# A state-space layer beside a mixture of experts: expert pairs move into scan group 0, slot scatters go by column, and POOL makes seven of the products dt*u*B

## What is computed

```
# ssm: 512 channels, 16 states each
xz = xn @ in_proj.T;  x, z = split(xz)            # no gate function on z
x  = silu(causal_conv4(x) + conv_b)
dt, Bm, Cm = split(x @ x_proj.T, [128, 16, 16])
dt = softplus(dt @ dt_proj.T + 2 * dt_proj_b)
state[l] = exp(dt * A) * state[l-1] + dt * Bm * x # per channel and state
y  = sum_n(state * Cm) + x * D;  out = (y * z) @ out_proj.T
# moe: 64 experts, top 8 of softmax(xn @ gate.T), weights not renormalised
h = silu(xn @ w1[e].T) * (xn @ w3[e].T);  out += c[e] * (h @ w2[e].T)
```

## Time and profile before

| | us |
|---|---|
| median of 3 runs (508.74 to 509.46) | 508.83 |
| profiled execution | 509.57 |
| its span, first to last instruction | 507.4 |
| PE busy | 430.4 |
| DVE busy | 430.5 |
| ACT busy | 246.7 |
| POOL busy | 293.8 |
| mean granted PE clock, share of full | 0.915 |

### The profile page before, as it was taken

One profiled execution on the slowest core, in us unless ns is written; L12 is line 12 of the kernel. 1 busy time (PEld: TensorE's weight loads), 2 busy tenths in 40 slices (PEclk: granted clock), 3 DMA queues, 4 the chain that ended last, 5 costly groups with the idle time before them and its releaser, 6 DMA issues.

```text
span 507.4 us, 9083 instructions
## 1 busy us (share of the span) xinstructions
PE 430.4 (85%) x2136; PEld 304.8 (60%) x2136; DVE 430.5 (85%) x646; ACT 246.7 (49%) x469; POOL 293.8 (58%) x260
## 2 busy tenths in 40 slices
PE   1986969038889999999999997999999949887996
PEld 1732424011157888788787885788878835454754
DVE  5288999989989888898789795888888889999994
ACT  1245367032435655555455665565555632454560
POOL 2000678777756766666545434566766537777772
PEclk9989979655569999999999997999999989997999
DMA  8999399722249999999999997899999944333432
GB/s 278 428 427 424 126 381 398 268 94 103 103 135 310 314 330 348 333 316 314 317 324 312 324 322 268 257 319 326 327 329 331 327 152 122 103 115 106 124 105 88
DMA packets 55417, 132.29 MB, mean 261 GB/s; under 512 B 7616, under 2 KB 11712, under 8 KB 53344
## 3 DMA queue, kind: packets, MB, share of 16 engines
q1 hardware_dynamic: 49248, 115.21, 65.6%
q0 software_dynamic: 6144, 16.79, 10.3%
HBM read 88.39 MB, written 43.58 MB: 260 GB/s over the span
## 4 chain that ended last, share of the span: by engine, by line
SPq 26%; POOL 18%; PE 15%; issue 15%; DVE 12%; DMA 12%; ACT 1%; POOLq 1%; DVEq 0%; ACTq 0%
POOL slot_x L329 13%; SPq L260 10%; SPq L261 6%; DMA slot_x<-bc 5%; DVE bank L572 5%; DMA slot_y<-x_sb 5%; PE bank L1004 4%; SPq L236 4%; SPq L264 3%; SPq L267 3%; PE bank L1015 2%; PE bank L1031 2%; DVE dbu L565 2%; PE bank L974 2%; DVE hc L578 2%
## 5 line engine op out<-in xcount | busy, mean ns | idle before, releaser
L337 POOL TENSOR_TENSOR dbu<-dtu,bc 128x512 f32 x80 | 101.9, 1274 | 99.5 <-DVE bank L572 86.8
L329 POOL DMA_INDIRECT slot_x<-x_sb,slot x64 | 68.8, 1075 | 68.2 <-DMA slot_x<-bc 49.0
L572 DVE TENSOR_TENSOR_SCAN bank<-dA,dbu 128x512 f32<-128x512 f32 x68 | 90.1, 1325 | 10.4 <-POOL dbu L337 1.7
L756 ACT ACTIVATE dA<-dt_sb,a_neg 128x512 f32<-128x512 f32 (+1 forms) x68 | 49.4, 727 | 66.3 <-DVE bank L572 66.1
L572 DVE TENSOR_TENSOR_SCAN bank<-bank,dbu 128x512 f32<-128x512 f32 x60 | 73.8, 1230 | 5.8
L782 ACT COPY x_sb<-bank 128x512 f32<-128x512 f32 x66 | 38.6, 585 | 75.0 <-DMA slot_y<-x_sb 72.7
L1004 PE MATMUL bank<-x_sb,wring 128*128 128x128 f32 x528 | 67.9, 283 | 0.1
L1004 PEld LDWEIGHTS bank<-x_sb,wring 128*128 128x128 f32 x528 | 64.8, 199 | 1.1 <-issue 0.5
L578 DVE TENSOR_TENSOR hc<-bank,bc 128x512 f32<-128x512 f32 x90 | 61.8, 686 | 1.4 <-POOL hp L344 0.3
L756 ACT ACTIVATE bank<-dt_sb,a_neg 128x512 f32 x60 | 41.7, 695 | 9.6 <-DVE bank L572 9.6
L592 DVE SCALAR_TENSOR_TENSOR gt<-th,bank 128x256 f32<-128x256 f32 x65 | 27.0, 416 | 22.5 <-ACT th L776 22.1
(11 more groups left out here) (180 smaller groups left out, 796.5 us busy)
## 6 DMA issues: line engine op xcount, KB each, us to landing
wring<-w_moe SPq DMA_DIRECT2D x64, 384.0 KB, 4.5
slot_y<-x_sb SPq DMA_DIRECT2D x66, 256.0 KB, 4.8
slot_x<-bc SPq DMA_DIRECT2D x16, 1024.0 KB, 22.1
xT<-w_moe SPq DMA_DIRECT2D x32, 384.0 KB, 4.5
win<-w_moe SPq DMA_DIRECT2D x32, 384.0 KB, 4.7
bc<-bc_dram SPq DMA_DIRECT2D x8, 1024.0 KB, 15.9
xg<-slot_x SPq DMA_DIRECT2D x32, 256.0 KB, 4.6
xT<-slot_x SPq DMA_DIRECT2D x16, 256.0 KB, 4.9
```

Of the source, the lines that this page charges most:

```text
L329: pool.indirect_dma_start(slot_x, bass.IndirectOffsetOnAxis(ap=slot[:, t * K + k:t * K + k + 1], axis=0), x_sb[:, t, :], None).then_inc(sc ...
L337: nc.gpsimd.tensor_tensor(dbu[:, j], at(dtu, g), bc[:, bass.ds(n, 1), 0].rearrange("p a l -> p (a l)"), ALU.mult).then_inc(dbu_ok, 1)
L572: nc.vector.tensor_tensor_scan(H[:], dA[:, j] if fall is None else fall, dbu[:, j], 0.0, ALU.mult, ALU.add).then_inc(scan_ok, 1)
L756: nc.scalar.activation(dA[:, j] if fall is None else fall, at(dt_sb, g), ACT.Exp, scale=a_neg[:, bass.ds(g, 1), bass.ds(n, 1)].rearrange(" ...
```

## The change

`EARLY` is 16, `GT` is G - 3 = 5. What it does, stage by stage:

- **Scatters** go by slot column: k = 7 for all 8 tiles first (the lowest slots), then k = 6, and so on. Each column has a semaphore; when it has landed, POOL raises `cols_ok`.
- **Early pairs.** DVE and PE work out for the first 16 pairs how many columns each needs (`low`, `lowest`, `reach`, `need`: four small operations on DVE, two on PE). `load_early` on SP reads that number into a register and waits for that many columns, then loads the rows. Worked out from the reference's inputs, pairs 0 to 15 need 1, 2, 3, 4, 4, 4, 4, 5, 5, 6, 6, 6, 6, 6, 7 and 7 columns.
- **Group 0** gets 12 pairs: from state 4 on, one `hidden` per scan step (`AHEAD0` = 4). It has one `sum_states` product on PE per scan step, three in pair step 0 and one in each later one. After scatter 36, and after every fourth from there, POOL makes the product dt*u*B for an odd state (`spread_odd`, states 1 to 13), each after the scan before it.
- **Groups 1 to 4** have the other 52 pairs: light, light, heavy, light. **Groups 5, 6 and 7** have none, so the last stage has 48 scan steps instead of 32, all with `spread_u` on DVE. `combine` begins at step 12 of them and takes in all 8 tiles; DVE copies the last two output tiles.
- The copies of z for groups 4 to 7 (`keep_z`) stand ahead of group 0. The load of `wout` moves from the preamble to the last stage, and that of x for the residual (`x_sb`, 1 MiB) from the last stage to the end of group 0; `xTs` and `ysb` take the room of `wx` and `wout`.

```diff
+EARLY = 16
-        hc_first = whole + [wdt[:], xg[:, 0]..., wx[:]...] + [mask, prob, key] + [hp[:], hc[:, 0], hc[:, 1]]
+        hc_first = [hc[:, 0], hc[:, 1]] + [f[:].rearrange("p t e -> p (t e)") for f in (prob, key)] + [dA[:, 1]] + hps[::-1]
...
-        G1, GH, G2, G3 = 1, DT - 1, G - 2, G - 1
+        G1, GH, GT, G3 = 1, DT - 1, G - 3, G - 1
+        RING0, AHEAD0, LAST = len(hc_first), 4, 3 * NS
+        FROM0, EACH0 = 36, 4
...
 @block.sync
-            sp.dma_start(wout[:], w_out.rearrange("(t p) n -> p t n", p=P)).then_inc(ld_wout, 16)
...
+            def load_early(p):
+                c = sp.value_load(need[0:1, p:p + 1], min_val=1, max_val=K)
+                sp.wait_ge(cols_ok, c)
+                load_x(p, p % 4)
...
-            sp.wait_ge(scat, 16 * NT * K)
-            sp.wait_ge(acc_ok, 3 * PART + C)
-            for i in range(4):
-                load_x(i, i)
+            for p in range(4):
+                load_early(p)
+            sp.wait_ge(sp_v, SP_STEPS * G)
+            for p in range(LIGHT):
+                sp.wait_ge(ye_ok, p + 1 + C)
+                load_w(p + 2, (p + 2) % 4)
+                sp.wait_ge(yc_ok, p + 1 + C)
+                store_y(p, p % 2)
+                sp.wait_ge(t_ok, p + 1)
+                load_early(p + 4)
+            sp.wait_ge(cols_ok, K)
+            sp.dma_start(x_sb[:], x_t).then_inc(ld_res, 16)
...
 @block.gpsimd
-            for t in range(NT):
-                for k in range(K):
-                    pool.indirect_dma_start(slot_x, ..., x_sb[:, t, :], None).then_inc(scat, 16)
+            def spread_odd(n):
+                pool.wait_ge(bc_ld[n // 4], 32)
+                pool.wait_ge(sp_v, SP_STEPS * G)
+                pool.wait_ge(scan_ok, n - 1 + C)
+                nc.gpsimd.tensor_tensor(dbu[:, 1], dtu[:, 0], bc[:, n, 0], ALU.mult).then_inc(dbo_ok, 1)
+            for c in range(K):
+                k = K - 1 - c
+                for t in range(NT):
+                    if c and t == NT // 2:
+                        arrived(c - 1)
+                    i = c * NT + t - FROM0
+                    if i >= 0 and i % EACH0 == 0:
+                        spread_odd(2 * (i // EACH0) + 1)
+                    pool.indirect_dma_start(slot_x, ..., x_sb[:, t, :], None).then_inc(scat[c], 16)
...
 @block.vector
+            def first(n):
+                if n % 2 and n < NS - 1:
+                    dve.wait_ge(dbo_ok, n // 2 + 1)
+                else:
+                    dve.wait_ge(dbv_ok, n // 2 + 1 + n % 2)
+                scan(0, n, n % 2, dA_light(n))
+                if n >= AHEAD0:
+                    hidden(n - AHEAD0, n % 2)
+                if n < NS - 1 and (n % 2 or n == NS - 2):
+                    spread_u(0, n + 1, 1 - n % 2)
+                if n >= RING0:
+                    dve.wait_ge(acc_ok, n - RING0 + 1 + C)
+                times_c(0, n, n % 2, hc_first)
...
 @block.scalar
+            for n in range(AHEAD0 + 1):
+                decay(0, n, n % 2, dA_light(n))
+            for m in range(LIGHT):
+                n = m + AHEAD0
+                take_x(m, m % 2)
+                decay((n + 1) // NS, (n + 1) % NS, (n + 1) % 2, dA_light(n + 1))
+                tanh(m, m % 2)
+                take_y(m, m % 2, m // 2)
...
 @block.tensor
-            for n in range(NS - 2):
-                sum_states(0, n, hc_first, PART if n % PART == PART - 1 else 2 if n == NS - 3 else 0)
+            for m in range(LIGHT):
+                step(m // 4, m % 4)
+                for n in (m + 2,) if m else range(3):
+                    sum_states(0, n, hc_first, 1)
...
-            for n in range(NS // 2):
-                sum_states(G2, n, hc_end, ...)
+            for s in range(LAST):
+                n, i = s % NS, s % 4
+                sum_states(GT + s // NS, n, hc_end, PART if n % PART == PART - 1 else 0)
...
+                if COMB <= s < COMB + 4 * NT:
+                    combine((s - COMB) // 4, (2 * i, 2 * i + 1))
```

More of the change, by code:

```diff
@@ L88, in program @@
         tau = sb("tau", [E, TILES])
+        lim = sb("lim", [K, EARLY])
+        low = sb("low", [P, K])
+        lowest = sb("lowest", [K, 1])
+        reach = sb("reach", [K, EARLY])
+        need = sb("need", [1, EARLY], I32)
         pars = sb("pars", [P, DT, NPAR])
@@ L181, in program @@
         sp_x, sp_s, sp_c, sp_ln, sp_v, a_exp, small = map(sem, "sp_x sp_s sp_c sp_ln sp_v a_exp small".split())
-        scat, ld_res = sem("scat"), sem("ld_res")
+        scat = [sem(f"scat{k}") for k in range(K)]
+        cols_ok, ld_res = sem("cols_ok"), sem("ld_res")
         dA_ok, dbu_ok, dbv_ok, scan_ok, hc_ok, hp_ok, acc_ok, y_out, yz_ok = map(
@@ L288, in steps @@
                     store_y(p, i % 2)
-            with sp.Fori(0, PAIRS // 4 - 1) as O:
+            with sp.Fori(LIGHT // 4, PAIRS // 4 - 1) as O:
                 steps(O)
@@ L495, in _ @@
                 weigh(t)
+            dve.wait_ge(pe_r, 7)
+            nc.vector.tensor_copy(need[:], PS[4][0:1, 3 * P:3 * P + EARLY]).then_inc(rt, 1)
             dve.wait_ge(a_exp, 1)
@@ L596, in hidden, with pair0 @@
                                                bank[:, 2 * INTER:4 * INTER], ALU.mult, ALU.mult).then_inc(hh_ok, 1)
-            def pair0(g, q, count, ring, after=None):
+            def pair0(g, q, count, after=None):
                 for j in range(2):
                     n = 2 * q + j
-                    if n % PART == 0 and g and (n >= RING or g == G3):
+                    if n % PART == 0 and (n >= RING or g > GT):
                         dve.wait_ge(acc_ok, g * NS + n - RING + PART + C)
@@ L610, in pair0 @@
                         spread_u(after[0], 0, 0)
-                    times_c(g, n, j, ring)
-            for q in range(NS // 4):
-                dve.wait_ge(bc_ld[q], 32)
-                if q == 0:
+                    times_c(g, n, j, hc_end)
+            def first(n):
+                if n % 4 == 0:
+                    dve.wait_ge(bc_ld[n // 4], 32)
+                if n == 0:
                     spread_u(0, 0, 0)
-                    pair0(0, 0, 0, hc_first)
-                else:
-                    pair0(0, 2 * q - 1, 0, hc_first)
-                    pair0(0, 2 * q, 0, hc_first)
-            pair0(0, QG - 1, 0, hc_first, ())
+                if n % 2 and n < NS - 1:
+                    dve.wait_ge(dbo_ok, n // 2 + 1)
+                else:
+                    dve.wait_ge(dbv_ok, n // 2 + 1 + n % 2)
+                scan(0, n, n % 2, dA_light(n))
+                if n >= AHEAD0:
+                    hidden(n - AHEAD0, n % 2)
+                if n % 4 == 3 and n < NS - 1:
+                    dve.wait_ge(bc_ld[n // 4 + 1], 32)
+                if n < NS - 1 and (n % 2 or n == NS - 2):
[3 more added lines that the diff above has]
+                times_c(0, n, n % 2, hc_first)
+            for n in range(NS):
+                first(n)
             def light(g, p):
@@ L747, in _ @@
                 nc.scalar.activation(sp_l[:, g], sp_l[:, g], ACT.Ln).then_inc(sp_ln, 1)
+            for g in range(4, G):
+                keep_z(g)
             act.wait_ge(sp_v, SP_STEPS * 2)
@@ L757, in decay @@
                     "p a l -> p (a l)")).then_inc(dA_ok, 1)
-            for n in range(NS):
-                decay(0, n, n % 2)
-                if 11 <= n < 15:
-                    keep_z(n - 7)
             def take_x(p, i):
@@ L860, in _ @@
                         nc.scalar.activation(diag[:, t % 2 * K + k], ident[:], ACT.Copy, scale=c8[:, t, k:k + 1]).then_inc(dg_ok, 1)
-            for t in range(4, NT - 1):
+            for s in range(LAST - 2, LAST):
+                decay(GT + s // NS, s % NS, s % 2)
+            for t in range(4, NT - 2):
                 act.wait_ge(o_ps, t - 3)
@@ L1113, in _ @@
                     project_out(t, k)
-            combine(NT - 2, range(K))
             pe.wait_ge(yz_ok, G)
```

159 lines of the change are left out of this document (82 added, 77 removed).

## The result

| | before | after |
|---|---|---|
| median, us | 509.07 (508.74 to 509.46, 4 runs) | 520.57 (518.22 to 523.52, 4 runs) |
| ratio | | 1.0228 (95% interval 1.0175 to 1.0281) |
| span of the profiled execution | 507.4 | 518.9 |
| PE, DVE, ACT, POOL busy | 430.4, 430.5, 246.7, 293.8 | 437.0, 434.6, 249.5, 271.2 |
| mean granted PE clock | 0.915 | 0.927 |

The change makes the kernel 2.3% slower. The forecast was 522.1 us, 1.5 above what was measured.

What follows compares the result with a forecast made beforehand. PE and SP were taken to bound the pair stage, DVE group 0 and the last stage. Span 507.4 - 24.2 (step 12 earlier) + 37.5 (longer last stage) = 520.7, giving 522.1 us; range 513 to 528.

Steps and rivals of the forecast that it cites:

- signs of being wrong: Step 12 before 155, last-stage scans closer than 2.5 us, or the 52 later pairs not taking 219.75 us.
- The last stage, +41.8: Last stage, first to last scan: 16 more scan steps and one more finish_group on DVE, 122.9 us against 81.1.
- Scan 0 at 106.5: Start of group 0: four small DVE operations added in the preamble, taken as 0.8 us; scan 0 starts at 106.5.
- The chain to step 2: Start of group 0: POOL's product after scan 0, then hidden of pair 0 at 120.2; step 2 at 123.
- the bound of 127: Latest start of pair step 2 in group 0, if PE's clock is still at half in step 1.
- The pace, 4.50 us: Group 0, ten pair steps: 3.94 us plus 0.56 for SP's register load; bounds 3.94 and 5.1.
- 52 later pairs 219.75 unchanged: Pair steps 12 to 63, from step 12's fetch to the last stage: 219.75 us, as in the kernel before.
- The end, 6.8: From the start of the last finish_group to the end: 6.8 us instead of 11.1; saved 4.3, bounds 2 to 5.5.
- Rival 1: Faster: group 0 takes the pairs at DVE's pace, steps about 3.1 us; 505.9 us; chance 0.15.
- Rival 2: No change: group 0 at PE's pace, 3.95 a step, step 2 at 116; 509.6 us; chance 0.06.
- Rival 3: DMA bounds more than SP: 4.85 us per step in group 0, x's load adds 3.2; 528.8 us; chance 0.16.
- Rival 4: No overlap: columns hold SP's queue in group 0 until about 155, step 12 at 202; span 555; chance 0.03.

Runs made afterwards that it cites:

- e1: The changed kernel with SP waiting for columns as constants instead of reading each number into a register; ratio to the kernel before 1.0136 (1.0109 to 1.0162).
- e10: The changed kernel with SP's numbers of columns read into registers before the first round, waits for columns kept; ratio to the kernel before 1.0101 (1.0006 to 1.0197).
- the kernel with late products: The changed kernel with 12 of the last stage's 48 products dt*u*B on POOL instead of DVE; ratio to the kernel before 1.0202 (1.0153 to 1.0251).
- e4: The changed kernel with POOL's wait for group 0's 14th sum moved to the first addition of two steps; ratio to the kernel before 1.0163 (1.0120 to 1.0206).

## Why the prediction was right, point by point

The time is well inside the range, and the account of the two ends, one group's scans paid at the end against pairs taken early, is what the trace shows. Between them it is partly luck: step 12 started 7.3 us before the forecast, and one of the signs of being wrong came true, the 52 later pairs did not take 219.75 us.

**The last stage, +41.8: right.** 48 scans in 122.93 us, to the hundredth the 47 x 2.54 + 3 x 1.18 of the forecast; gathers end ahead of DVE. This term decides the sign.

**Scan 0 at 106.5: right** (106.45), by luck. DVE reached its first `spread_u` at 104.23 instead of 103.94, so the four small operations cost about 0.3 us and not 0.8. The rest is that operation itself, which took 2.19 us beside POOL's product. In the other kernels with this preamble scan 0 starts anywhere from 104.84 to 109.70.

**The chain to step 2: 3.3 us too late in this execution.** I put it at 123, it was 119.67. The step that failed is "it starts when scan 0 ends". Scan 1 does not wait for a product begun after scan 0:

```profile
104.57 1.29 POOL L367 TENSOR_TENSOR dbu<-dtu,bc 128x512 f32<-128x512 f32 x1
```

The product of state 1 began at 104.57, before scan 0, because `spread_odd(n)` waits for scan n - 2, the last reader of its buffer, and not for the scan before it, as the section on the change has it (`scan_ok` counts from `C` = 2, so n - 1 + `C` means n - 1 scans). So scans 1 and 3 came at once after DVE's own work (108.54, 113.17), states with a product of POOL took 2.09 us and not 2.55, and `hidden` of pair 0 was done at 117.8, not 120.2. PE's clock was full from 110 on (window above, 1.00).

But this profile shows the early case. From scan 0 to step 2 it has 13.22 us, and so have four other profiles of kernels with this start (13.21 or 13.22). Seven have 15.9 to 18.1, around the 16.5 of the forecast. In the five POOL's product of state 1 starts at least 1.8 us before scan 0, in the seven from 0.1 us before it to 2.0 after it. One of the seven is the profile of the changed kernel on the third chip:

```profile
108.73 1.23 DVE L629 TENSOR_TENSOR_SCAN bank<-bank,dbu 128x512 f32<-128x512 f32 x1 [1.37 <-POOL dbu L367]
...
115.25 1.23 DVE L629 TENSOR_TENSOR_SCAN bank<-bank,dbu 128x512 f32<-128x512 f32 x1 [2.02 <-POOL dbu L367]
```

Scans 1 and 3 wait for POOL there, `hidden` of pair 0 is done at 119.86, and step 2 starts at 123.49 after PE has run at half clock from 119.9 to 123.9 (granted 0.50), which is what the bound of 127 was for. In all twelve the case goes with how far POOL is in its scatters when DVE comes to group 0; in none does the product wait for scan 0.

**The pace, 4.50 us: right for SP, wrong for PE.** SP's stores are (161.00 - 116.02) / 10 = 4.50 us apart, with 2.5 us of waits in 118 to 170 us. That it hits the forecast is in part luck: less the waits the round is 4.25, since a read is 0.3 to 0.4 us and not 0.56, and other profiles of the same program have 4.53 to 4.84. That the read costs SP time, and the kernel with it, held. But "step: 4.50" put SP's round on PE, and PE took 41.05 us for ten steps, 4.1 each: the first four at its own 3.95, some of the later ones held by `take_y`, which waited 17.3 us in all for stores of y to land. The loads ahead covered the difference. That makes step 12 4.0 us early.

**"52 later pairs 219.75 unchanged": 3.4 too small.** Two things are in it; neither was in the sum. Step 12 to 13 takes 6.75 us and not 4.7, by POOL's wait and the half clock behind it (`fetch` 1.06 us instead of 0.60 at 167.47). These 2.0 us have nothing to do with SP's round: without any read in the rounds the step takes 6.59 (e1) and 6.58 (e10), and with the wait moved 4.11. The other 1.4 us come after step 13, in 216.44 us against 215.05. Without the read (e1) they are 214.17, so this part looks like SP's lag, paid late. On the third chip the changed kernel shows it sooner: 42.82 us for steps 2 to 12, and 214.26 after step 13. A stage that hands over a queue in arrears does not leave the next as it was, but most of the 4.0 us that PE won against the forecast in group 0 was not paid back.

**The end, 6.8: 1.1 too small, and 0.9 before it.** PE had idled, and its last work ran at half clock:

```profile
508.95 2.05 PE L1043 MATMUL bank<-wring,ident 128*128 128x512 f32 x2 [1.06 <-DVE wring L635]
512.56 3.78 PE L1158 MATMUL bank<-wout,u 128*128 128x256 f32 x8 [1.57 <-DVE u L643]
```

The four projection products took 3.78 us where I had 1.9, and the last sum 2.05 instead of 1.02.

So the sum came out 1.8 us high with a span of 518.9: -3.3 and -4.0 before step 12, +3.4, +0.9 and +1.1 behind it. Three terms were off by more than the total, so that the total lies so close is luck.

**The rivals.** Rival 1 (DVE's pace) fails: DVE was 6.60 of 10 us busy, and steps took 4.1 us, not 3.1. Rival 2 (PE's pace, early start) has the start half right (119.67 between its 116 and my 123) and the pace nearly: 4.1 against 3.95. Its step 12 at 155.5 was 5.2 too early, mine at 168.0 7.3 too late. Rival 3 (DMA) is refuted by the bytes: 362 GB/s in the stage, 388 once the reads are gone. This is also above the 353 that I had used as the best rate with pairs. The Trainium skill (DMA: Bandwidth & Descriptors, Measured) has roughly 358 for a core whose neighbour streams too and 425 for one core alone; both rates measured here lie between the two. Rival 4 fails: SP waited for a column once, for 2.9 us, ahead of its first store (116.02), and never after 118 us. POOL did not wait for DVE from state 7 on, as I had it, so the last scatter was issued at 148.34 and not near 165.

## What to carry to other kernels

Work that moves to a stage with a free engine leaves another stage, and what stays behind there runs at that stage's own limit: price both ends, here 31.5 us won against 41.8 lost. Which of two engines comes late at the start of a stage can differ from one execution to the next, so one profile may not show the usual case. A queue that issues DMAs one by one has a round of its own; count its register loads like work, and read constants of the loop before it. Where one engine has loads in hand, a slower queue shows little at first and then as waits in the next stage, so add up over both.

## What the runs showed of the hardware

- A register load on SP costs 0.33 to 0.54 us of a round with four DMAs, of 4.2 to 5.0 us, and 0.3 to 0.4 us when SP's waits are taken off. The Trainium skill (DMA: Bandwidth & Descriptors, Latency and other measured facts) puts the floor of such a load at about 600 ns; the measured slopes lie under it.
- A DMA share of 0.97 to 1.03 from 125 to 160 us went with anything from 335 GB/s (the changed kernel on the third chip) to 389 (reads ahead and the wait at the addition); the share alone doesn't say that the DMA engines are the limit.
- DVE operations with both inputs in SBUF take longer beside a product of POOL: in the changed kernel the first `spread_u` takes 2.19 us (104.23) and not 0.67, with POOL's product at 104.57, and the scan at 163.11 takes 2.07, where one that reads its decay from PSUM stays at 1.23 (111.08) beside a product of POOL (111.20). In the kernel with late products it was 1.48. The Trainium skill (SBUF — State Buffer, SBUF: two separate sides) says that such operations of the two engines lock a shared port and that the later one waits. These rows agree in kind, though not on which is the later one: the `spread_u` at 104.23 started before POOL's product and still waited. The price was 0.25 to 1.5 us each. I had priced a product on POOL as free for DVE.
- After an idle stretch of PE of 4 us (e4, 181.02) its products ran at half clock (granted 0.50), 3.75 us instead of 1.95 for sixteen.
